# Second layer of a two-layer network: which engine mixes the value heads, VectorE or POOL

## The reference

```
q = (x @ Wq).reshape(b, t, h, dh).transpose(0, 2, 1, 3)
k = (x @ Wk).reshape(b, t, h, dh).transpose(0, 2, 1, 3)
gl_v = (x @ Ws).reshape(b, t, h, e)
wv = _topk_mask(gl_v, SEL) * jax.nn.sigmoid(gl_v)
xv = jnp.einsum('btd,edk->btek', x, Wv)
v = jnp.einsum('bthe,btek->bhtk', wv, xv)
scores = jnp.einsum('bhid,bhjd->bhij', q * scale, k)
probs = jax.nn.softmax(scores, axis=-1)
attn = jnp.einsum('bhij,bhjd->bihd', probs, v)
gl_o = (x @ Wd).reshape(b, t, h, e)
mask_o = _topk_mask(gl_o, SEL)
out = jnp.einsum('bthe,bthk,ekd->btd', mask_o, attn, Wo)
```

## Time and profile before

| | |
|---|---|
| median of 3 runs | 2792.52 us (2789.43 to 2797.73) |
| profiled execution | 2793.39 us, its span 2791.7 us |
| PE busy | 2336.8 us (84% of the span) |
| DVE busy | 1882.4 us (67%) |
| ACT busy | 1695.5 us (61%) |
| POOL busy | 1862.2 us (67%) |

### The profile page before, as it was taken

The page is one execution under the profiler, slowest core; times in us unless marked ns, Lnnn a source line. Parts: engine busy times, 40 slices in busy tenths (PEclk is TensorE's granted clock), DMA queues, the critical chain, the costliest instruction groups (busy, mean ns, idle before and its releaser), DMA issues. The chain is left out here.

```text
span 2791.7 us, 31646 instructions
## 1 busy us (share of the span) xinstructions
PE 2336.8 (84%) x10169; PEld 1176.0 (42%) x10169; DVE 1882.4 (67%) x3123; ACT 1695.5 (61%) x2439; POOL 1862.2 (67%) x1978
## 2 busy tenths in 40 slices
PE   5667778777777777785888899989999999999996
PEld 2222323232333323223555445545555555555543
DVE  5888989898888988764333356566666656566574
ACT  1778888979888888990122264545554545555445
POOL 0555577787878687874577302959595958677776
PEclk8668787878788787777899899999999999999998
DMA  3000000000000010115699500000000000000000
GB/s 105 16 1 1 18 16 16 18 15 19 8 19 15 10 23 3 24 17 112 192 272 242 121 1 1 1 1 16 8 16 9 16 8 16 8 9 1 1 8 16
DMA packets 94103, 98.98 MB, mean 35 GB/s; under 512 B 18897, under 2 KB 90705, under 8 KB 93905
## 3 DMA queue, kind: packets, MB, share of 16 engines
q1 hardware_dynamic: 70752, 73.99, 9.2%
q0 software_dynamic: 23152, 22.68, 4.6%
HBM read 69.98 MB, written 26.66 MB: 35 GB/s over the span
## 5 line engine op out<-in xcount | busy, mean ns | idle before, releaser
L1049 POOL TENSOR_TENSOR TT<-TT,SS 128x512 f32<-128x512 f32 x512 | 651.8, 1308 | 221.8 <-ACT SS L978 221.2
L1816 ACT ACTIVATE PR<-S,NM 128x512 f32<-128x512 f32 x512 | 344.8, 685 | 263.5 <-DVE NM L2000 263.5
L2000 DVE TENSOR_REDUCE NM<-S 128x2 f32<-128x1024 f32 x256 | 301.6, 1219 | 134.0 <-PE S L1706 134.0
L734 DVE TENSOR_SCALAR TT<-SC 128x1024 f32<-128x1024 f32 x256 | 311.4, 1216 | 72.7 <-POOL TT L1049 44.6
L464 PE MATMUL OB<-TT,VAL 128*17 128x512 f32 x1024 | 343.6, 774 | 4.8 <-ACT TT L986 4.8
L736 DVE SCALAR_TENSOR_TENSOR SS<-SC,TT 128x1024 f32<-128x1024 f32 x256 | 313.5, 1225 | 20.6 <-issue 1.8
L1054 POOL DMA_INDIRECT slot_tokens<-TID,IDX x224 | 229.0, 1022 | 101.1 <-issue 67.1
L1717 PE MATMUL TP<-ident,PR 128*128 128x128 f32 x2048 | 272.9, 276 | 19.9 <-DVE TT L2005 15.4
L1717 PEld LDWEIGHTS TP<-ident,PR 128*128 128x128 f32 x2048 | 235.9, 142 | 109.9 <-issue 69.3
L2005 DVE COPY TT<-TP 128x512 f32<-128x512 f32 x256 | 176.1, 688 | 143.4 <-PE TP L1717 139.6
L1822 ACT ACTIVATE TT<-TP 128x512 f32<-128x512 f32 x256 | 153.1, 598 | 177.3 <-PE TP L1717 173.4
(11 more groups left out here) (296 smaller groups left out, 4084.1 us busy)
## 6 DMA issues: line engine op xcount, KB each, us to landing
TT<-w_gu SPq DMA_DIRECT2D x64, 384.0 KB
TT<-w_dn SPq DMA_DIRECT2D x64, 128.0 KB
XL<-x SPq DMA_DIRECT2D x8, 512.0 KB
stream<-V SPq DMA_DIRECT2D x4, 1024.0 KB, 10.4
rows<-XL SPq DMA_DIRECT2D x8, 512.0 KB
TT<-w_dn SPq DMA_DIRECT2D x64, 64.0 KB
XS<-stream SPq DMA_DIRECT2D x8, 512.0 KB, 4.5
X<-x SPq DMA_DIRECT2D x7, 512.0 KB
```

Of the source, the lines that this page charges most:

```text
L734: dve.tensor_scalar(tt[:, :, mt, :], SC[mt % 2][:], 0.0, None, ALU.max)
L1049: ins = pool.tensor_tensor(tt, tt, ss, ALU.add)
L1816: act.activation(PR[s % 2][h2][:], S[s % 2][:, h2, :], ACT.Exp, bias=NM[:, s % 2, h2:h2 + 1], accum_out=SM[:, pair % 2, j, h2:h2 + 1]).the ...
L2000: dve.tensor_reduce(NM[:, s % 2, :], S[s % 2][:], AX, ALU.max, negate=True).then_inc(sems["peak"], 1)
```

## The change

For batches 0 to 6 the second head of each pair goes from POOL to DVE, as it was for batch 7 alone. POOL's loop takes one head of a pair, and the tables `PREP_2` and `PREP_2_FIRST` get eight entries each for DVE's two parts. For `PREP_2` they stand in twos 6 and 7 of the run ahead and in twos 0 to 3 of the kind-2 run itself. The waits follow: PE waits for both semaphores, ACT waits for both before it overwrites `XV`, DVE waits for POOL's count alone before it overwrites `WV`, and `weigh_own` waits for the batch's own expert products.

```
-    (1, 0, A, "keys2", 2), (1, 1, A, "queries2", 3), (1, 2, A, "keys2", 3))
+    (1, 0, A, "keys2", 2), (1, 1, A, "queries2", 3), (1, 2, A, "keys2", 3),
+    (0, 6, D3, "weigh_own", 0), (0, 7, Z, "sum_own", 0), (0, 7, D3, "weigh_own", 1), (1, 0, Z, "sum_own", 1),
+    (1, 0, D3, "weigh_own", 2), (1, 1, Z, "sum_own", 2), (1, 2, D3, "weigh_own", 3), (1, 3, Z, "sum_own", 3))
...
+    (1, 0, D3, "weigh_own", 0), (1, 1, Z, "sum_own", 0), (1, 1, D3, "weigh_own", 1), (1, 2, Z, "sum_own", 1),
+    (1, 2, D3, "weigh_own", 2), (1, 3, Z, "sum_own", 2), (1, 4, D3, "weigh_own", 3), (1, 5, Z, "sum_own", 3))
...
-                    if kind == 2 and b < B - 1:
-                        pe.wait_ge(sems["vh"], v.next("vh", 2))
-                    elif kind == 2:
-                        pe.wait_ge(sems["vh"], H1 * b + pair + 1)
-                        pe.wait_ge(sems["vh_own"], pair + 1)
+                    if kind == 2:
+                        pe.wait_ge(sems["vh"], PAIRS1 * b + pair + 1)
+                        pe.wait_ge(sems["vh_own"], PAIRS1 * b + pair + 1)
...
                 if j == 0 and b > 0:
-                    act.wait_ge(sems["vh"], H1 * b)
+                    act.wait_ge(sems["vh"], PAIRS1 * b)
+                    act.wait_ge(sems["vh_own"], PAIRS1 * b)
...
                     if b > 0:
-                        dve.wait_ge(sems["vh"], H1 * b)
+                        dve.wait_ge(sems["vh"], PAIRS1 * b)
...
                 if pair == 0:
-                    dve.wait_ge(sems["experts_in"], NT * B)
+                    dve.wait_ge(sems["experts_in"], NT * (b + 1))
...
-                for h in (2 * pair, 2 * pair + 1) if b < B - 1 else (2 * pair,):
+                for h in (2 * pair,):
```

More of the change, by code:

```diff
@@ L1283 @@
     (1, 0, D3, "mix_values", 2), (1, 0, D3, "mix_values", 3), (1, 0, C3, "queries2", 1), (1, 1, A, "keys2", 1),
-    (1, 1, C3, "queries2", 2), (1, 2, A, "keys2", 2), (1, 2, Z, "queries2", 3), (1, 2, C3, "keys2", 3))
+    (1, 1, C3, "queries2", 2), (1, 2, A, "keys2", 2), (1, 2, Z, "queries2", 3), (1, 2, C3, "keys2", 3),
+    (1, 0, D3, "weigh_own", 0), (1, 1, Z, "sum_own", 0), (1, 1, D3, "weigh_own", 1), (1, 2, Z, "sum_own", 1),
+    (1, 2, D3, "weigh_own", 2), (1, 3, Z, "sum_own", 2), (1, 4, D3, "weigh_own", 3), (1, 5, Z, "sum_own", 3))
 OUT_1_LAST = table((0, 2, Z, "product_out1", 0), (0, 2, C3, "product_out1", 1), (0, 3, A, "product_out1", 2),
```

## The result

The changed kernel took 2836.39 us in the median of 4 runs (2832.94 to 2843.94), against 2793.61 us for the kernel before (4 runs): a ratio of 1.0154, 95% interval 1.0135 to 1.0173. It is slower by 42.8 us. Forecast were 2841 us, and 2808 to 2868 as the range.

A forecast was written before the change was run, and what follows sets the result against it. PE was taken to bound stage three. Added DVE delays of +62.5 us, -19.1 for waits for `XN` and +4.8 net clock gave +48.2 us, so 2841 us was forecast, range 2808 to 2868.

The forecast's parts named there:

- Each place named with a cost: Where DVE's new weighings and sums delay PE, walked in batch 2 in program order: together 9.65 us a batch.
- DVE hides all of it: Rival: only PE's waits for `XN` and their three clock falls go, giving 2769 us, faster; chance 0.05.
- nothing is hidden: Rival: all 117 us of DVE's added work land on PE, about 2895 us; chance 0.03.
- DVE spreads its lateness: Rival: DVE falls behind and catches up freely, only 3.3 us a batch surface, about 2794 us; chance 0.09.
- sum 1 and weighing 2: DVE's second sum ahead of the peaks and third weighing ahead of the copy out of `BK`: 3.8 us a batch.
- Sum 3: DVE's fourth sum ahead of the peaks makes copy `XT`, and so PE's use of `BK`, late: 1.7 us a batch.
- half a batch: Batch 0's entries stand in its own run's twos 0 to 5, not walked: 4.5 us, between 0 and 9.65.
- the 62.5 of the sum: DVE's added cost on PE: 58 us for batches 1 to 6 plus 4.5 for batch 0.
- I take all five waits as gone: POOL's relief removes PE's five waits for `XN`: -19.1 us; three clock falls removed give back another 4.8.
- the waits for `XN` stay: Rival: POOL's gates are late for another reason while DVE's delays come as computed, 2865 us; chance 0.11.
- a fourth less of the walk: Range allowance on the place-by-place count of DVE's delays, a fourth less or a third more.
- One fall for each of six batches: Added PE waits of over 3 us each bring a granted-clock fall: 9.6 us, between 0 and 20.

The follow-up runs named there:

- e3: Changed kernel with one `PREP_2` entry, the third weighing, moved from ahead of the copies of `BK` and `TP` to between the `TP` copies: 2813.21 us, ratio 1.0072.
- e4: Changed kernel with nearly all of DVE's new entries between the two copies of `TP`, spread over eight twos: 2775.49 us, ratio 0.9940.
- e7: e3 with the second and third sums also moved, from ahead of the peaks to between the `TP` copies: 2810.69 us, ratio 1.0037, other occasion and chip.
- e1: Kernel before, with the second head of each pair mixed by no engine in batches 0 to 6: 2769.1 us, ratio 0.9912.
- e2: Changed kernel with POOL still mixing the second heads too, into a tile nobody reads: 2842.53 us, ratio 1.0182.
- e6: e4 with POOL mixing the second heads too, into a tile nobody reads: 2829.79 us, ratio 1.0112, other occasion and chip.

## Why the prediction was right, and where it was not

**The bound and the cost.** PE sets the time, and DVE's added 114 us (117 in the prediction) reach it only through instructions that stand behind them in a fixed order. Each place named with a cost lengthened its two, and the sum for a batch was 8.3 us for 9.65 computed. e3, e4 and e7 show that place and order, not DVE's load, decide: the same 56 instructions cost 51.5 us in one order and under 6 in another. The rivals "DVE hides all of it" and "nothing is hidden" are both out for the order that the change has. "DVE spreads its lateness" would have left 3.3 us a batch.

**A reading that was wrong.** Against "DVE hides all of it" I wrote that DVE's idle times are pieces of 0.4 to 1.3 us into which no 1.8 or 2.4 us fits. The kernel before has longer ones, between the two copies of a two; this one stands in two 0 of the stretch that I walked:

```profile
2038.69 0.69 DVE L2005 COPY TT<-TP 128x512 f32<-128x512 f32 x1 [1.91 <-PE TP L1717]
```

They did not matter for the order that the change has, which puts nothing into them. In e4, which uses them, the same instructions cost under 6 us.

**Sizes that were off.** The dearest place, sum 1 and weighing 2, was put at 3.8 us and measured 2.88. I took from the wait only the idle of 0.38 before the peaks. The weighing there took 1.49 us, not the mean of 1.80 that I had kept (-0.3); the copy `RB<-RS` ran 0.43 us where it had been 0.75 beside POOL's mixing (-0.3); and the idle of 0.22 before the copy to `AT`, which I left out, took its share. Sum 3 was 1.26 for 1.7. Batch 0, taken at half a batch without a walk, came out at 4.33 for 4.5. Batch 6, taken like the others, lost 5.9. All this is 51.5 us for the 62.5 of the sum.

That the median came within 5 us of the forecast is partly luck. The terms of the prediction give 62.5 + 9.6 - 23.9 = 48.2 us; the profiled executions give 51.5 + 7.4 - 24.6 + 2.0 + 6.0 = 42.3, and the last two, batch 7 and the very end, were in no step of mine. Without them the difference would be 34 us, 14 under the forecast but still slower and inside the range. The range itself is not what its reason says: a fourth less of the walk is 16 us, and its lower end is 33 us below the forecast.

**The gain.** The step "I take all five waits as gone" held in the result, -24.6 us for the -23.9 put down. Its reason was only half right. I had written that POOL's relief removes them; e1 shows that it does so alone, but e2 shows that the added lateness of PE removes four of the five without any relief. The rival "the waits for `XN` stay" at 2865 us had DVE's delays in full and the waits in full. In e2, where POOL is not relieved at all, that did not happen: with the delays in, only batch 1's wait stayed.

**Contention.** The prediction took the weighing at its mean and counted POOL's loss as harmless. In the changed kernel it is harmless: for batch 2 POOL takes up the statistics 0.08 us after they are ready (1973.06 for 1972.98), having idled 0.80 us for them. In e6, where POOL is the late engine, a loss of about 4 us a batch went to PE in full. The Trainium skill's "GPSIMD Engine Reference", section 8, Key points, says that POOL contends with VectorE instructions of two SBUF inputs; the trace agrees, and in both directions: 1696 against 1496 ns for the weighing, 1.8 to 2.1 against 0.73 us for an addition beside it.

**The clock.** One fall for each of six batches was assumed, for 9.6 us; there were four, for 7.4 us. The reason given, new waits of over 3 us, did not come true: the longest new wait at that place was 2.1 us, and the falls came all the same in four of six batches. That the term was of the right size is luck.

## What to carry to other kernels

When work is moved to an engine with idle time, look not for the share of idle time but for its pieces, and at what stands behind the new instruction in that engine's queue: here it was nearly free between two copies that wait for the bounding engine, and cost its whole length ahead of a copy that frees a bank. Two terms of a sum that are both waits of one engine need not simply add: here lateness from one source hid the other, so measure each alone and both together before crediting either. Of an engine that is given work, check too what its new instructions do to the engine beside it.

## What the runs showed of the hardware that I had not expected

- The same wait of PE, 1.73 and 1.72 us behind the same instructions, was followed by a fall of the granted clock to 0.50 in batch 2 and by none in batch 3. So here the wait's length alone does not tell whether the clock falls.
- A DVE multiplication of 128x1280 with two inputs in SBUF holds up single POOL instructions by 1.1 to 1.4 us and is itself held up by 0 to 0.6 us. It is 1.49 to 1.53 us without any POOL mixing beside it.
- Most twos without a new wait agree to 0.01 us between kernels, on either chip, with single exceptions of up to 0.14 where no clock fell. So differences of tenths of a microsecond in one two could be read from a single profiled execution each, while the medians of the same kernel on the two occasions differed by 7 us.
